# State space layers: the z product moved from the input stage into the scan, its gate applied to turned sums

## The reference, cut to what matters

```
xz = xn @ in_proj                      # 512 -> 2 * 1024
x_in, z = split(xz)
u  = silu(causal_conv(x_in))           # 4 taps for each channel
dt_r, B, C = split(u @ x_proj)         # 64, 16, 16
dt = softplus(dt_r @ dt_proj + b)
h_t = h_{t-1} * exp(dt_t * A) + dt_t * u_t * B_t      # 1024 x 16 states
y_t = sum_n h_t * C_t + u_t * D
out = (y * silu(z)) @ out_proj         # then the layer's gate; layer 2 adds its input
```

## Time and profile before

| | |
|---|---|
| median of 3 runs | 6384.57 us (6381.27 to 6394.48) |
| the profiled execution, its own time | 6369.16 us |
| its span, first to last instruction | 6367.0 us |
| granted TensorE clock, mean | 0.966 |
| PE, DVE, ACT, POOL busy | 86%, 74%, 66%, 39% of the span |
| `ssm_inputs`, layer 2 and 3 | from about 2255 to 2935, and from 4273 to 4973 |
| `scan`, layer 2 and 3 | from about 2937 to 4271, and from 4976 to 6285 |

### The profile page before, as it was taken

How to read it: one execution, slowest core, us unless ns; L and a number is a source line. 1 busy time by engine, 2 the same in 40 slices (tenths; PEclk the granted TensorE clock), 3 DMA queues, 4 the chain that set the end, 5 groups by cost and what they waited for, 6 DMA issues and landing times. The chain is left out here.

```text
span 6367.0 us, 85962 instructions
## 1 busy us (share of the span) xinstructions
PE 5507.0 (86%) x30568; PEld 3508.8 (55%) x30568; DVE 4685.2 (74%) x5708; ACT 4205.5 (66%) x6216; POOL 2483.0 (39%) x1098
## 2 busy tenths in 40 slices
PE   8989999997899989995788888879999578888884
...
GB/s 223 190 147 71 86 79 81 100 34 146 100 44 49 40 117 141 144 135 182 153 160 165 158 165 158 160 109 88 145 145 147 172 150 153 159 160 157 158 146 177
DMA packets 571129, 842.72 MB, mean 132 GB/s; under 512 B 100544, under 2 KB 239936, under 8 KB 570704
## 3 DMA queue, kind: packets, MB, share of 16 engines
q1 hardware_dynamic: 559248, 811.92, 43.6%
...
## 5 line engine op out<-in xcount | busy, mean ns | idle before, releaser
L1910 POOL TENSOR_TENSOR scan_hC<-scan_h,scan_Crep 128x1024 f32<-128x1024 f32 x1024 | 2396.0, 2375 | 2429.0 <-DVE scan_h L2143 2418.4
L2074 ACT ACTIVATE scan_a<-scan_dt,scan_A 128x512 f32<-128x512 f32 x2048 | 1368.7, 697 | 93.6 <-DVE scan_h L2143 76.7
L1944 PE MATMUL scan_y<-ident,scan_hC 128*128 128x128 f32 x8192 | 1107.3, 278 | 285.4 <-POOL scan_hC L1910 279.8
L1944 PEld LDWEIGHTS scan_y<-ident,scan_hC 128*128 128x128 f32 x8192 | 897.5, 141 | 674.9 <-POOL scan_hC L1910 626.4
L2143 DVE TENSOR_TENSOR_SCAN scan_h<-scan_a,scan_carry,scan_h 128x512 f32<-128x512 f32 x1024 | 1216.6, 1260 | 8.8 <-ACT scan_a L2074 5.4
L2143 DVE TENSOR_TENSOR_SCAN scan_h<-scan_a,scan_h 128x512 f32<-128x512 f32 x1024 | 1155.1, 1200 | 53.2 <-ACT scan_a L2074 52.5
L2050 ACT COPY scan_h<-scan_drive 128x1024 f32<-128x1024 f32 x1024 | 1042.3, 1018 | 148.8 <-PE scan_drive L1932 136.0
L1932 PE MATMUL scan_drive<-scan_Bd,scan_dT 128*128 128x256 f32 x4096 | 748.0, 305 | 124.7 <-ACT scan_h L2050 73.2
L1932 PEld LDWEIGHTS scan_drive<-scan_Bd,scan_dT 128*128 128x128 f32 x4096 | 556.3, 192 | 177.7 <-issue 92.3
L861 DVE CUSTOM_DVE_ANT_0 att_sm<-att_S,att_mneg 128x1024 f32<-128x1024 f32 x512 | 621.9, 1215 | 14.5 <-POOL att_mneg L787 14.2
L919 ACT ACTIVATE att_pr<-att_sm,att_nmax 128x1024 f32<-128x1024 f32 x512 | 590.6, 1153 | 55.9 <-DVE att_nmax L861 43.4
...
## 6 DMA issues: line engine op xcount, KB each, us to landing
scan_dT<-scratch_dtuT SPq DMA_DIRECT2D x512, 256.0 KB, 6.3
scratch_dtuT<-ssmin_dT SPq DMA_DIRECT2D x128, 512.0 KB, 3.4
...
att_q<-scratch_q_split SPq DMA_DIRECT2D x256, 128.0 KB, 4.4
att_k<-scratch_k_split SPq DMA_DIRECT2D x256, 128.0 KB, 4.6
...
scratch_z<-ssmin_zt SPq DMA_DIRECT2D x128, 256.0 KB, 2.1
...
```

Source lines behind the costliest of these rows:

```text
L1910: nc.gpsimd.tensor_tensor(hC[k % 2][:], of, Crep[:, 2 * p:2 * p + 2, :], ALU.mult).then_inc(s["scaled"].handle, 1)
L1944: last = nc.tensor.matmul(y[j][:, t, :], hC[k % 2][:, i, t * P:(t + 1) * P], ident[:], start=(p == 0 and i == 0 and t == 0), stop=False, i ...
L2074: nc.scalar.activation(a[(2 * k + i) % 3][:], dt[j][:], ACT.Exp, scale=A[:, m, 2 * p + i:2 * p + i + 1]).then_inc(s["decayed"].handle, 1)
```

## The change

`ssm_inputs` no longer makes z: its 16 z products for each sequence, their `Silu`, their stores and the weight `Wz` go, and `xT` is stored to memory instead (2 transfers of 1 MB for each sequence). `scan` loads `xT` of a half (1 MB) and the 128 columns of `Wz` of a block (256 KB), and makes z of the block on PE, channels on partitions, into a new PSUM bank `Z`. ACT takes tanh(z/2), DVE makes (tanh + 1) * z, which is 2 z sigmoid(z); the sum y is copied by ACT to SBUF, turned by PE into the same bank `Z`, and DVE multiplies it by 0.5 and by what it made of z. The result has channels on partitions as the output product wants it, so `turn_g` and `copy_g` go, and in the last half `turn_late`, `turn_last` and `copy_late` too. `y` has one PSUM buffer where it had two. The scratch for POOL's descriptors is set to 4096, where nothing was given before.

```diff
@@ ssm_inputs: z products leave PE, ACT, SP; xT is stored
+            def store_xT(it):
+                for h in range(2):
+                    rows.ready(sp, it, h)
+                    sp.dma_start(scr["xT"][it, :, :, h * HALF:(h + 1) * HALF], xT[it % 2][:, :, h * HALF:(h + 1) * HALF]
+                                 ).then_inc(xT_out[it % 2].handle, 16)
...
             for it in range(B):
                 if gather is None and it + 1 < B:
                     rows.load(sp, it + 1)
+                store_xT(it)
                 for m in range(IB + 1):
                     if it and m < IB:
                         store_dT(it - 1, m)
...
-                for n in range(Z_FIRST):
-                    take_z(n)
                 w(act, "proj", it + 1)
...
                 for m in range(IB):
-                    if m == 4:
-                        for n in Z_MID:
-                            product(2 * IB + n)
-                    product(2 * IB + z_with(m))
                     if m >= 4:
@@ scan, PE
+            def z_product(blk, some):
+
+                if 0 in some:
+                    pe.wait_ge(Wz_in.handle, Wz_in.at(16 * (blk + 1)))
+                    if blk % IB == 0:
+                        pe.wait_ge(xT_in.handle, xT_in.at(16 * (blk // IB + 1)))
+                    if blk >= 1:
+                        w(pe, "gated", blk)
+                for kt in some:
+                    last = nc.tensor.matmul(Z[:], Wz[:, kt, :], xT[:, kt, :], start=(kt == 0), stop=(kt == KT - 1))
+                if KT - 1 in some:
+                    last.then_inc(s["z_made"].handle, 1)
+
+            def turn_y(blk):
+                w(pe, "y_copied", blk + 1)
+                w(pe, "z_ready", blk + 1)
+                for t in range(4):
+                    last = nc.tensor.transpose(Z[:, t * P:(t + 1) * P], yS[:, t, :], ident[:])
+                last.then_inc(s["y_turned"].handle, 1)
...
                 if k + 4 < UNITS_ALL:
                     make_drive(k + 4)
                 n, step = tile_at(k)
-                if step == 1:
-                    turn_g(n, 0)
-                if step == 5:
-                    turn_g(n, 1)
+                blk, p = k // UNITS, k % UNITS
+                if p == 1 and 0 <= k - 2 < UNITS_ALL:
+                    turn(k - 2)
                 if step is not None and 7 <= step < 15:
                     product(n, step - 7)
-                if 0 <= k - 2 < UNITS_ALL:
+                if p != 1 and 0 <= k - 2 < UNITS_ALL:
                     turn(k - 2)
...
+                if p == 3 and 1 <= blk < BLOCKS:
+                    turn_y(blk - 1)
+                if p in (5, 6) and blk < BLOCKS:
+                    z_product(blk, range(2 * p - 10, 2 * p - 8))
@@ scan, ACT
+            def copy_y(blk):
+                w(act, "y_full", blk + 1)
+                if blk >= 1:
+                    w(act, "y_turned", blk)
+                nc.scalar.copy(yS[:], y[:]).then_inc(s["y_copied"].handle, 1)
+
+            def bend_z(blk):
+
+                w(act, "z_made", blk + 1)
+                if blk >= 1:
+                    w(act, "gated", blk)
+                nc.scalar.activation(zs[:], Z[:], ACT.Tanh, scale=0.5).then_inc(s["z_bent"].handle, 1)
...
                 if k < UNITS_ALL:
                     decay(k)
+                if k % UNITS == 2 and UNITS <= k < UNITS_ALL + UNITS:
+                    copy_y(k // UNITS - 1)
                 if k + 4 < UNITS_ALL:
                     lay(k + 4)
...
+                if k % UNITS == 0 and UNITS <= k < UNITS_ALL + UNITS:
+                    bend_z(k // UNITS - 1)
@@ scan, DVE
+            def make_z(blk):
+
+                w(dve, "z_bent", blk + 1)
+                nc.vector.scalar_tensor_tensor(out=zs[:], in0=zs[:], scalar=1.0, in1=Z[:], op0=ALU.add, op1=ALU.mult
+                                               ).then_inc(s["z_ready"].handle, 1)
+
             def gate(blk):
-                w(dve, "y_full", blk + 1)
-                dve.wait_ge(z_in.handle, z_in.at(16 * (blk + 1)))
-                product = zg[:] if blk < LAST else gl[:, blk - LAST]
-                nc.vector.tensor_tensor(product, y[blk % 2][:], zg[:], ALU.mult).then_inc(s["gated"].handle, 1)
+                w(dve, "y_turned", blk + 1)
+                w(dve, "z_ready", blk + 1)
+                if 1 <= blk < LAST:
+                    dve.wait_ge(g_out.handle, g_out.at(16 * blk))
+                product = g[:] if blk < LAST else gl[:, blk - LAST, :]
+                nc.vector.scalar_tensor_tensor(out=product, in0=Z[:], scalar=0.5, in1=zs[:], op0=ALU.mult, op1=ALU.mult
+                                               ).then_inc(s["gated"].handle, 1)
...
-                if k % UNITS == 4 and UNITS <= k < UNITS_ALL + UNITS:
+                if k % UNITS == 2 and UNITS <= k < UNITS_ALL + UNITS:
+                    make_z(k // UNITS - 1)
+                if k % UNITS == 5 and UNITS <= k < UNITS_ALL + UNITS:
                     gate(k // UNITS - 1)
```

More of the change, by code:

```diff
@@ L1325, in ssm_inputs @@
         ea, dt = ([sb(f"{n}{k}", [P, T]) for k in range(4)] for n in ("ea", "dt"))
-        zt = [sb(f"zt{k}", [P, HALF]) for k in range(2)]
         dT = [sb(f"dT{k}", [P, 2, HALF]) for k in range(2)]
@@ L1360, in ssm_inputs @@
         assert len(entries) % 4 == 0
-        weights_in = [core.count(f"weights_in{n}") for n in range(4)]
+        weights_in = [core.count(f"weights_in{n}") for n in range(3)]
         block = ctx.enter_context(nc.Block())
@@ L1410, in _ @@
                 for m in range(IB):
-                    zs = {0: [z_with(k) for k in range(4)], 2: Z_MID, 4: [z_with(k) for k in range(4, 8)]}.get(m, ())
-                    for n in zs:
-                        store_z(it, 2 * IB + n)
-                        if it == B - 1 and m == 4:
-                            store_dT(it, zs.index(n))
+                    if it == B - 1 and m == 4:
+                        for n in range(4):
+                            store_dT(it, n)
                     w(sp, "dt", it * IB + (m + 1))
@@ L1420, in _ @@
             for k in range(2):
-                for stores, n in ((dT_out, 128), (uD_out, 64), (z_out, 128)):
+                for stores, n in ((dT_out, 128), (uD_out, 64), (xT_out, 16)):
                     sp.wait_ge(stores[k].handle, stores[k].at(n * B))
@@ L1759, in scan @@
         LOOP = UNITS_ALL + UNITS + 1
-        turn_bank = [drive[:, P // 2 * k:P // 2 * (k + 1), :].rearrange("p t n -> p (t n)").rearrange("p (m t) -> p m t", t=P)
-                     for k in range(2)]
-        late = [y[0][:].rearrange("p t d -> p (t d)")] + [a[k][:] for k in range(3)]
+        late = [drive[:, P // 2 * k:P // 2 * (k + 1), :].rearrange("p t n -> p (t n)") for k in range(2)] + [a[k][:] for k in range(2)]
         where = lambda blk: (blk // (2 * IB), blk // IB % 2, blk % IB)
@@ L1885, in _ @@
                     sp.dma_start(Wo[:], io[f"out_w{layer}"].rearrange("(k p) f -> p k f", p=P)).then_inc(Wo_in.handle, 16)
-                if blk < BLOCKS:
-                    load_z(blk)
                 if change:
                     load_C(half, 2)
-                if m % 2 == 1 and 0 <= tile + 1 < REST:
-                    load_og(tile + 1, 0)
+                if blk + 1 < BLOCKS:
+                    load_Wz(blk + 1)
+                    if change:
+                        load_xT(half)
                 if blk + 2 < BLOCKS:
@@ L1895, in _ @@
                     load_C(half, 3)
+            for n in range(REST, TILES):
+                store_o(n)
             sp.wait_ge(g_out.handle, g_out.at(16 * LAST))
@@ L2003, in product_late @@
                 if IB - 1 in some:
-                    w(pe, "last_copied", 9)
+                    w(pe, "gated", BLOCKS)
                 for m in some:
-                    last = nc.tensor.matmul(late[j], gTl[:, j, m, :], Wo[:, m, :], start=(m == 0), stop=(m == IB - 1))
+                    last = nc.tensor.matmul(late[j], gl[:, m, j * P:(j + 1) * P], Wo[:, m, :], start=(m == 0), stop=(m == IB - 1))
                 if IB - 1 in some:
```

250 lines of the change are left out of this document (89 added, 161 removed).

## The result

| | before | after |
|---|---|---|
| median of 4 runs | 6385.94 us | 6817.45 us (6797.03 to 6826.37) |
| ratio, 95% interval | | 1.067 (1.064 to 1.070) |
| profiled execution, span | 6367.0 us | 6795.2 us |
| granted TensorE clock, mean | 0.966 | 0.922 |

6.7% slower: the sign and the range held (the forecast's own range, 6600 to 6820, by under 3 us), the forecast of 6715 was 102 us short. By stages, from the first x product, the first product of POOL and the first gather of the stage behind, in the two traces: `ssm_inputs` went from 706.5 to 641.3 us in layer 2 (both counted from their first x product) and from 733.0 to 652.5 in layer 3 (counted from its first gather), 146 less; `scan` from 1305.6 to 1579.6 and from 1280.7 to 1580.9, 574 more; the rest within 3 us. Forecast were -156 and +484 (490, less 6 at the scan's end).

The account below looks back on a forecast made before the run. PE bounds the input stage and DVE nearly fills the scan, where z's place makes DVE stall: +490 scan, -156 input stages, -6 scan ends, +328 on 6384.6 makes 6713, said as 6715; own range 6600 to 6820, with rivals 6535 to 6840.

Parts of the forecast that it names:

- Where z stands bounds the scan, and busy time doesn't show it: Scan: PE's z waits about 2 us for DVE's gate in nearly all blocks; DVE idles over 400 us for ACT's decay.
- The two stalls: Scan: DVE stands still 1.96 or 2.08 us after z's first half, another 0.72 to 1.70 after its second.
- z, 4 passes at 13.74 / 32 = 0.43 us, 1.72: Scan, PE: half of z's product for a block takes 1.72 us, in the chain between gate and decay.
- Input stage -156: `ssm_inputs`: 49 + 73 - 28 - 16 = 78 us a layer saved, 156 in all; bounds 100 and 240.
- Part B's chain of 45.5 us: Input stage: without z, part B is a chain through the one buffer DTP, 45.5 us a sequence where it took 63.7.
- The clock's share of it: Part B: lower PE clock lengthens dt products by some 1.9 us; 7 us a sequence, 28 a layer.
- the stores of xT, taken at 16 us in each layer: Input stage: 2 MB ahead of the `scratch_dtuT` stores on SP's queue make ACT wait, 6.5, 6.5 and 3 us.
- DVE +75 for `make_z`: Scan: the new DVE operation takes 0.6 us a block, 0.5 in the first half, where POOL was the bound.
- Edits costed at nothing: Scan queues and buffers: `Wz` load, `xT` load ahead of C's last quarter, and single `y`, each taken at 0.
- (b): Clock stays at 0.50 all through part B, and PE comes late into p = 5: 6829 us; chance 0.13.
- (a): Scan: PE slips ahead, only the gate's wait counts, ACT's slack takes z's second half: 6554 us; chance 0.16.
- (c): Scan: z's 3.4 us a block vanish in PE's idle time, only DVE's 75 us is added: 6298 us; chance 0.08.

Follow-up runs that it names:

- wait_filled: Changed kernel with twelve transposes of zeros added on PE after the turn of p = 5, before z waits for the gate; 6728.1 us.
- store_late: Changed kernel with the two stores of xT behind the stores of part A on SP's queue instead of ahead of them; 6801.8 us.
- spread: Changed kernel with z in four single parts over four units behind the gate, and turn, make_z and output pieces moved to even PE's time; 6377.5 us.
- half_the_z_work: Changed kernel with two of the four parts of z's product left out; 6584.1 us.
- spread_xT_parts: The `spread` kernel with xT loaded in two parts of 512 KB, the first ahead of C's last quarter, and the stores of xT late; 6323.2 us.

## Why the prediction was right in sign and 100 us short

- *Where z stands bounds the scan, and busy time doesn't show it.* Right. PE waited 1.0 to 1.9 us for the gate in 126 blocks, DVE stood 528.8 us for the decay, gates are 22.5 to 26 us apart. Its figure for the wait before is misread: the earlier trace rows gives 53.2 us for the halves without carry, not "in all"; in all it was 62.0.
- *The two stalls.* Right in mechanism and size: first half of the scan 22.52 us a block (forecast 18.6 + 3.9), pairs with carry 23.18 + 25.06 = 48.24 (40.4 before + 7.8), pairs without 22.59 + 24.30 = 46.89 (38.7 + 8.4 = 47.1).
- *"z, 4 passes at 13.74 / 32 = 0.43 us, 1.72".* **The step that failed.** It prices z at the full clock. I had the fall of the clock in part B and did not ask the same of the wait that I put ahead of z in the scan: there z's first half took 3.3 to 3.8 us in 42 blocks. `wait_filled` prices that at 89 us, of the 102 that were missing (by the profiled executions 67 of 100). With the wait filled the scans are 504 us longer than before, forecast 484.
- *Input stage -156.* Measured -146, in part by luck, as errors in its terms offset each other. Part B's chain of 45.5 us at the full clock was right: it took 46.5 where fills kept the clock up. The clock's share of it was 8.5 us, not 7, as the dt products were long in seven tiles of eight, not in four: part B 55.0 us for my 52.5. In the second sequence part A rose by 8.5 us (72.05 to 80.55; I had 1.8 and 6.5). But the stores of xT, taken at 16 us in each layer, come out at 14 in layer 2 and 2 in layer 3 by `store_late`.
- *DVE +75 for `make_z`.* Right for blocks with carry, 0.6 us each in `spread`. Without carry it is 0.7, and in the first half 1.1, where 0.5 was forecast: ACT is late there even with z spread.
- *Edits costed at nothing.* The turn of a block's first unit does wait for `copy_y`, 82.9 us in all, but the forecast without it gives the time of the regular blocks, so it seems to delay nobody there; no run tests it alone. The xT load made no wait of POOL for C in the changed kernel, but 49.4 us of PE's in `spread`, and POOL's for C once xT went ahead. The gather's stage is 79.7 us for 78.0. Table loads 0, right.
- *The rivals.* (b) came nearest in number, 6829, by luck for the most part. Its first half did happen, as the clock was at 0.55 all through part B, but the input stages fell short by 10 us and not by 50; its second half didn't, as PE had to wait for the gate in all 126 blocks and so was not late into p = 5. (a) fell with `half_the_z_work`: the second half of z counts. (c), 6298 because z fits into PE's idle time, was true of PE's sum and false of this order; `spread_xT_parts`, with another order and the stores late, got there but for 25 us.
